# First layer's edge pass: turned one-hots of the first 16 chunks made on chip, sums cleared earlier

## What is computed

```python
x_src, x_dst, e = node_embeddings[src], node_embeddings[dst], edge_emb[edge_type]
att_in = concatenate([x_src, x_dst, e, task_rep])
edge_delta = tanh(gelu(att_in @ att_W1 + att_b1) @ att_W2 + att_b2)
edge_weight = 1.0 + edge_scale * edge_delta
...
agg = segment_sum(messages * edge_weight, dst)
deg = segment_sum(edge_weight, dst)
```

## Time and profile before

| | us |
|---|---|
| median of 3 runs | 3634.98 |
| lowest, highest | 3631.04, 3635.08 |
| profiled execution, its own time | 3634.52 |
| span of its trace | 3632.7 |
| busy: PE, DVE, ACT, POOL | 2852.6, 2641.7, 1922.9, 2197.2 |

### The profile page before, as it was taken

The page is one execution under the profiler, slowest core; times in us unless marked ns, Lnnn a source line. Parts: engine busy times, 40 slices in busy tenths (PEclk is TensorE's granted clock), DMA queues, the critical chain, the costliest instruction groups (busy, mean ns, idle before and its releaser), DMA issues. The chain is left out here.

```text
span 3632.7 us, 59741 instructions
## 1 busy us (share of the span) xinstructions
PE 2852.6 (79%) x14869; PEld 1755.7 (48%) x14869; DVE 2641.7 (73%) x7559; ACT 1922.9 (53%) x6218; POOL 2197.2 (60%) x2264
## 2 busy tenths in 40 slices
PE   2578619999989699577777768599999998888885
PEld 1444305555556455354555535466666654333332
DVE  9899828999987455688888854599999955444444
ACT  0277705555552154377777743378887844333333
POOL 0687767777767532566666523677776312777774
PEclk9988859999999699699999989799999998565665
DMA  4334337888870488877776734777777634333335
GB/s 133 115 86 124 109 96 242 265 261 265 265 202 25 116 333 341 283 219 208 213 204 203 187 106 175 213 220 220 220 221 218 157 125 185 103 103 103 103 104 102
DMA packets 259351, 651.50 MB, mean 179 GB/s; under 512 B 65353, under 2 KB 114324, under 8 KB 252244
## 3 DMA queue, kind: packets, MB, share of 16 engines
q0 software_dynamic: 143184, 474.54, 44.1%
q1 hardware_dynamic: 115844, 173.14, 14.9%
HBM read 505.48 MB, written 145.31 MB: 179 GB/s over the span
## 5 line engine op out<-in xcount | busy, mean ns | idle before, releaser
L1976 POOL DMA_INDIRECT a_rows<-table,met x568 | 549.7, 968 | 280.9 <-issue 120.0
L3537 PE MATMUL ps<-rows_in,hot_w 128*128 128x256 f32 x832 | 444.8, 644 | 104.5 <-ACT hot_w L3499 57.6
L1275 POOL DMA_INDIRECT rows_in<-table,met x416 | 411.5, 989 | 144.1 <-issue 107.1
L3487 POOL DMA_INDIRECT rows_in<-table,met x416 | 403.9, 971 | 140.6 <-issue 120.0
L3562 DVE TENSOR_TENSOR xs<-xs,ps 128x256 f32 x416 | 175.3, 421 | 303.9 <-PE ps L3537 302.1
L778 POOL DMA_INDIRECT records<-rec,rows x283 | 323.5, 1143 | 101.7 <-issue 86.0
L3537 PEld LDWEIGHTS ps<-rows_in,hot_w 128*128 128x128 f32 x832 | 196.0, 289 | 353.4 <-ACT hot_w L3499 176.9
L3499 ACT ACTIVATE hot_w<-hot,met 128x128 f32<-128x128 f32 x416 | 166.8, 402 | 374.8 <-PE ps L3537 345.6
L2452 PE MATMUL ps<-a_rows,a_hot 128*128 128x260 f32 x1136 | 314.3, 402 | 23.5 <-DVE acc L2458 16.1
L1976 POOL DMA_INDIRECT xs<-table,met x264 | 255.6, 968 | 122.9 <-issue 54.5
L2458 DVE TENSOR_TENSOR acc<-acc,ps 128x520 f32 x416 | 287.5, 691 | 20.5 <-issue 15.0
(11 more groups left out here) (473 smaller groups left out, 6422.9 us busy)
## 6 DMA issues: line engine op xcount, KB each, us to landing
a_hot_t<-one_hots SPq DMA_DIRECT2D x104, 256.0 KB, 4.8
table<-stage SPq DMA_DIRECT2D x25, 1024.0 KB, 3.9
rows_in<-table,met POOLq DMA_INDIRECT x832, 3.8
dst_row<-slot_rows SPq DMA_DIRECT2D x52, 256.0 KB, 5.2
one_hots<-hot_t SPq DMA_DIRECT2D x52, 256.0 KB, 3.6
by_dst<-lo_rows SPq DMA_DIRECT2D x24, 512.0 KB, 4.6
by_dst<-dst_rows SPq DMA_DIRECT2D x24, 512.0 KB, 5.7
a_rows<-table,met POOLq DMA_INDIRECT x568, 3.8
```

Source lines behind the costliest of these rows:

```text
L1275: e.indirect_dma_start(self.rows[:, n % self.RING, 0:2 * D], None, self.table, bass.IndirectOffsetOnAxis(ap=self.b.met[:, n, R_SRC:R_SRC + ...
L1976: e.indirect_dma_start(self.row(n, 0, self.width), None, self.table, bass.IndirectOffsetOnAxis(ap=b.met[:, n, self.word:self.word + 1], ax ...
L3487: e.indirect_dma_start(self.rows[:, n % self.RING, :], None, self.table, bass.IndirectOffsetOnAxis(ap=self.b.met[:, n, R_REL:R_REL + 1], a ...
L3537: e.matmul(b.ps[:, n % self.BANKS, 0:D], self.hot_w[:, n % GRP_H, :], self.rows[:, n % self.RING, :], start=True, stop=True).then_inc(self ...
```

## The change

The changed kernel makes `hot_t` and `kind_t` of the first 16 chunks (two groups of eight) without memory. `first_hots` compares, on VectorE, the destination and type words of eight chunks with a row of numbers, which gives the one-hots the other way round (slots along partitions), in room lent by the tile `z`; `turn_first` transposes them on TensorE, 16 transposes of a group, into two PSUM banks; `keep_first` copies the two banks into `hot_t` and `kind_t` on ScalarE. The loads of `dst_row` and `type_row` begin with the third group. `acc` is cleared before VectorE waits for the records; for that `hi_hot` and `lo_hot`, whose room it takes, are laid out first, and the clearing waits for TensorE's last use of them. The second `sources` moves behind the copies of the slot rows (`decode_rest`). Cut to its core:

```diff
-        self.hi = sb("hi_hot", [P, RC, NT], BF16)
-        self.lo_hot, self.lo_b = sb("lo_hot", [P, 2, BLK, P], BF16), sb("lo_b", [P, RC], BF16)
+        self.hi, self.lo_hot = hots
+        self.lo_b = sb("lo_b", [P, RC], BF16)
...
     FIRST_CHUNKS = 48
-    DECODED_ROWS, DECODED_FIRST, DECODED_BANKS, DECODED = 13, 16, 18, 21
+    DECODED_ROWS, DECODED_FIRST, DECODED_BANKS, DECODED = 13, 18, 22, 25
...
             e.wait_ge(self.tiles, done[0])
+        e.wait_ge(self.moved, N_BLK)
+        e.memset(self.acc[:, :, :], 0.0)
+        self.between.all_stored(e)
         e.wait_ge(*self.put.at(self.placed_before(N_BLK)))
         e.wait_ge(b.s_met, 16)
...
         assert done[0] == self.DECODED_ROWS
+        settled()
+        self.messages.first_hots(e, 0, step)
         self.sources(e, step, settled, 0, self.FIRST_CHUNKS)
         assert done[0] == self.DECODED_FIRST
+        self.messages.first_hots(e, 1, step)
         step(e.scalar_tensor_tensor(met_f[:, :, R_KEY], ps[:, 0, 0:NCH], float(P), met_f[:, :, R_DST], ALU.mult, ALU.add))
         step(e.tensor_tensor(met_f[:, :, R_W], ps[:, self.WORDS + 1, 0:NCH], qf[:, :, WEIGHT], ALU.add))
         assert done[0] == self.DECODED_BANKS
+
+    def decode_rest(self, e):
+
+        b, done, met = self.b, [self.DECODED_BANKS], self.b.met
+
+        def step(last):
+            done[0] += 1
+            last.then_inc(self.tiles, 1)
+
+        def settled():
+            e.wait_ge(self.tiles, done[0])
         self.sources(e, step, settled, self.FIRST_CHUNKS, NCH)
         assert done[0] == self.DECODED
         settled()
...
-    BANKS = 1, 2
+    BANKS = 2, 5
...
+    FIRST_GROUPS, FIRST_BANKS = 2, ((4, 3), (7, 6))
...
+        early = self.z[:, :, :, :].rearrange("p k c f -> p (k c f)").bitcast(BF16)
+        at = self.FIRST_GROUPS * GRP_T * P
+        self.early_hot = early[:, 0:at].rearrange("p (c q) -> p c q", q=P)
+        self.early_kind = early[:, at:at + self.FIRST_GROUPS * GRP_T * 3 * ET].rearrange("p (c k y) -> p c k y", k=3, y=ET)
...
-            if g >= groups:
+            if g >= groups or g < self.FIRST_GROUPS:
                 continue
...
         b, w = self.b, self.w
+        for g in range(self.FIRST_GROUPS):
+            self.keep_first(e, g)
         for t in range(self.PAIRS + 2):
...
+    def first_hots(self, e, g, step):
+
+        b, chunks = self.b, slice(g * GRP_T, (g + 1) * GRP_T)
+        word = lambda w: b.met[:, chunks, w:w + 1].bitcast(F32)
+        step(e.tensor_tensor(self.early_hot[:, chunks, :], b.iota_b[:, :].unsqueeze(1).to_broadcast([P, GRP_T, P]),
+                             word(R_DST).to_broadcast([P, GRP_T, P]), ALU.is_equal))
+        for k in range(3):
+            last = e.tensor_tensor(self.early_kind[:, chunks, k, :], b.iota_b[:, 0:ET].unsqueeze(1).to_broadcast([P, GRP_T, ET]),
+                                   word(R_TYPE).to_broadcast([P, GRP_T, ET]), ALU.is_equal)
+        step(last)
+
+    def early_bank(self, g, k, rows):
+        return self.b.ps[0:rows, self.FIRST_BANKS[g][k], :].bitcast(BF16).rearrange("p (c q) -> p c q", c=GRP_T)
+
+    def turn_first(self, e, g):
+
+        b, ranking = self.b, self.ranking
+        e.wait_ge(ranking.tiles, (ranking.DECODED_ROWS + 2, ranking.DECODED_BANKS)[g])
+        for c in range(GRP_T):
+            e.transpose(self.early_bank(g, 0, P)[:, c, :], self.early_hot[:, g * GRP_T + c, :], b.ident_b[:, :])
+            last = e.transpose(self.early_bank(g, 1, 3 * ET)[:, c, :],
+                               self.early_kind[:, g * GRP_T + c, :, :].rearrange("p k y -> p (k y)"), b.ident_b[:, :])
+        last.then_inc(self.first_turned, 1)
+
+    def keep_first(self, e, g):
+
+        e.wait_ge(self.first_turned, g + 1)
+        e.copy(self.hot_t[:, g, :, :], self.early_bank(g, 0, P)).then_inc(self.hot_t_made, 1)
+        e.copy(self.kind_t[:, g, :, :], self.early_bank(g, 1, 3 * ET)).then_inc(self.hot_t_made, 1)
...
         self.slot_rows.tensor(e, (self.ranking.tiles, self.ranking.DECODED_ROWS))
-        e.wait_ge(self.ranking.tiles, self.ranking.DECODED_BANKS)
+        for g in range(self.FIRST_GROUPS):
+            self.turn_first(e, g)
         self.ranking.between.brought(e)
         fetch(0)
         for t in range(self.PAIRS + 3):
             if t + 1 < self.PAIRS:
                 fetch(t + 1)
+            if t == 1:
+                e.wait_ge(self.slot_rows.kept, 2)
             if t % 2 and t < self.PAIRS:
...
-            e.wait_ge(self.row_in[g % 2], 32 * (g // 2 + 1))
+            e.wait_ge(self.row_in[g % 2], 32 * ((g - self.FIRST_GROUPS) // 2 + 1))
...
         self.slot_rows.vector(e)
-        e.memset(self.acc[:, :, :], 0.0)
-        turned_hots(0)
+        self.ranking.decode_rest(e)
         for t in range(self.PAIRS + 4):
-            if t % 4 == 1 and t // 4 + 1 < NCH // GRP_T:
+            if t % 4 == 1 and self.FIRST_GROUPS <= t // 4 + 1 < NCH // GRP_T:
                 turned_hots(t // 4 + 1)
...
+        hots = sb("hi_hot", [P, RC, NT], BF16, film_ctx), sb("lo_hot", [P, 2, BLK, P], BF16, film_ctx)
         film_room = sb("film_room", [P, 6 * KD * 2 * D], F32, film_ctx)
         film, load_film = film_steps(b, film_ctx, w, film_room)
-        ranks = Ranks(b, film_ctx, back, film_room[:, :])
+        ranks = Ranks(b, film_ctx, back, film_room[:, :], hots)
```

6 lines of the change are left out of this document (3 added, 3 removed).

## The result

| | us |
|---|---|
| kernel before, median of 7 runs on the same chip | 3632.74 (3629.77 to 3638.46) |
| changed kernel, median of 7 runs | 3623.42 (3619.18 to 3626.28) |
| ratio, 95% interval | 0.9971 (0.9960 to 0.9983) |
| profiled execution: time, span | 3626.28, 3624.5 |

The change is a gain of 0.29%: by the ratio 10.5 us, with an interval of 6 to 14.5. The kernel before came out 2.2 us lower here than in its first three runs. A second set of runs of the same changed kernel gave 0.9973 (0.9963 to 0.9983).

The account below looks back on a forecast made before the run. Bound: the first layer's pass, by when GpSimd's gather 16 starts after a 10.81 us pause. Gather 16 at 542.3 in place of 550.61 saves 8.3: 3634.98 - 8.3 = 3626.7 us, range 3622.5 to 3630.5.

Parts of the forecast that it names:

- a microsecond won there is a microsecond of the kernel: First layer's pass: it ends by when gather 16 starts, gathers after it taking a steady 1.296 us each.
- Product L1435 and the gather beside it: VectorE product of 0.42 us at 552.48; the gather beside it took its usual 0.94, read as not held.
- The scatter beside L320: GpSimd scatter beside VectorE's long compare: 1.90 us in place of 0.94 to 1.01, taken as the nearest case.
- Compares ahead of gather 0: Four VectorE compares before GpSimd's release: 1.9 us, moving gather 0 from 519.83 to 521.7.
- Gather 0 beside the second compares: Second four VectorE compares run while first gathers are issued: cost 0.3 us, bounds 0 and 0.95.
- The rival in which it is locked out: GpSimd held by VectorE's compares: costs 1.1 us rather than 0.3, gain 7.5, time 3627.5; chance 0.12.
- Transposes: TensorE ahead of the first fetch: four took 0.41 us, so 16 take 1.64, ending at 526.1.
- Register load of 1.37 us: TensorE, between the transposes and the first fetch: adds 1.37 us, bringing the fetch to 527.5 in place of 536.58.
- GpSimd's own queue ends last at gather 16: First place free at 541.5, before GpSimd is ready at 542.3, so the 10.81 us pause is gone.
- Rows in time for the z: VectorE's first z due at 529.9; gather 1's rows land by 529.3, close but in time.
- places come free late: Rival: rows or group 3 loads late for VectorE's z; 1 to 3 us of new pause, 3627.7 to 3629.7; chance 0.14.
- the rival of a clock that stays low: TensorE stays at 1.2 GHz, paced by gathers; the 8.3 us are lost after 3.3 pairs, kernel slower; chance 0.04.

Follow-up runs that it names:

- e3: Changed kernel with the clearing of the sums put back behind the second sources, ahead of the first z; ratio to the kernel before 0.9979.
- e6: Changed kernel with the first sources ahead of both sets of compares and each group's wide transposes before its narrow ones; ratio to the kernel before 0.9963.
- e7: Changed kernel with only the first 8 chunks' one-hots made on chip, one group in place of two; ratio to the kernel before 0.9963.
- e4: Changed kernel with each group's 8 wide transposes made first, then its 8 narrow ones, in place of in turn; ratio to the kernel before 0.9969.
- e5: Changed kernel with the first chunks' sources ahead of both sets of compares; ratio to the kernel before 0.9958.
- e2: Kernel before with only the change's early clearing of the sums and the new layout; ratio to the kernel before 1.0000.
- e1_again: Changed kernel, unedited, run once more; ratio to the kernel before 0.9973.

## Why the prediction was right, and where it was not

- **The step that failed: "a microsecond won there is a microsecond of the kernel".** Gather 16 came 8.63 us earlier (forecast 8.3), but the pass got only 7.39 shorter. That is the prediction's own sign against itself: a pass less than 8 us earlier although gather 16 came 8 us earlier. The step rested on gathers of 1.296 us, "its own duration and gap and nothing else". The gap holds (0.30 us, and behind gather 16 never over 0.6); the duration does not. It follows which of VectorE's rows the gather starts behind, and after the change 14 more were hit: gathers 16 to 415 took 2.5 us more (519.44 against 516.98). Of this 1.2 came back between the last gather and the end. Why it did is open: passes of equal length had their last gathers 0.7 us apart. In the other runs the rate isn't one for one either (e3: 2.4 later, 1.2 longer; e6: 1.3 earlier, 1.8 shorter; e7: 1.7 later, 1.5 longer). In the nine profiles of whole kernels in the first table the pass is gather 16's start and 536.7 to 538.1 us, so the start of gather 16 sets the pass to within 1.4 us, not to one.
- **The misread row behind it.** Product L1435 and the gather beside it were read as a case in which nothing is held. That gather starts 0.63 us ahead of the product, and a gather ahead of its row isn't lengthened (none of 199). The scatter beside L320 starts with 1.07 us of the compare left, and its 1.90 us are 0.947 and 1.07 less 0.13, nearly to the hundredth. Both rows say the same.
- **Compares ahead of gather 0: right.** 1.23 and 0.69 us, overlapping, delay it by 1.87 (forecast 1.9). R_W ended at 8.39 (528.26 absolute), forecast 8.65.
- **Gather 0 beside the second compares: 0.3 forecast, nothing net.** It took 1.20 us, 0.19 above its 1.01 before. But the first 16 gathers took 20.27 us as before, where one other had been lengthened to 1.15; that is luck. The rival in which it is locked out to 0.95 us past the last compare wanted its end at 527.6; it ended at 526.92. The rival's mechanism is what the rows show, but only for the row under way, and its price of 1.1 us fell.
- **Transposes: mis-sized.** "Four took 0.41, so 16 take 1.64": they took 3.69. The row has four of one width; here two widths take turns, and e6 puts 1.7 us of the difference on that alternation (2.01 us when grouped, at the same clock of 0.50; still 0.4 above the forecast).
- **Register load of 1.37 us behind them: mis-sized the other way.** The fetch started 0.15 us after the last transpose (0.22 in e6), so the loads must have run beside them. The two errors nearly cancel, which is luck: first fetch 12.29, forecast 11.65; first z 14.65, forecast 14.05. They cost nothing, since the place was needed only when GpSimd came round.
- **GpSimd's own queue ends last at gather 16: right.** 26.13, forecast 26.45 (the 0.3 above is the difference), pause gone. e4, with the fetch 2.4 us earlier, left it at 26.14.
- **Rows in time for the z: wrong for two.** The first three waited for none, the fourth and fifth waited 1.61 and 1.47 us for gathered rows. In e5 the fifth came 1.3 us earlier and the pass gained nothing. It is the rival "places come free late" as far as its mechanism goes, without its price here; in the sets with late rows it is most of the story, and the prediction had no case for them.
- **Clearing costs nothing and is needed: right.** e2 and e3 show both halves; what it is needed for is 1.2 us of the pass.
- **ScalarE, SyncE: right.** Copies 1.01 and 1.00 us (at most 1.17), and the first loads went out at 13.55, 1.3 us sooner than thought.
- **Clock: right.** Low until 25.5, forecast 25.2 (541 less 515.85), and the rival of a clock that stays low fell in the changed kernel (1.00 in the steady window). Its mechanism exists: in e4, where TensorE ran further ahead of the gathers, the clock went back to 0.50 for some 7 us.
- **The time.** 3626.7 forecast, 3623.4 measured. Of the 3.3 us 2.2 are the kernel before, which came out lower in the larger set. The saving of 8.3 lies in the measured 6 to 14.5, and the medians differ by 9.3; of these the pass gives 7.4. That the total fits is partly luck: in the two profiles the ranking ended 4.0 us later and the rest behind the pass took 4.8 us less, and e1_again (first decoding row at 515.47) shows that the later ranking isn't the change's. The other error was in calling 0.2% the line: with 7 runs each the interval was 0.12% either way, so that there is a gain could be told more easily than the chances allowed. That it is over 0.2% isn't shown (0.17 to 0.40%).

## What to carry to other kernels

Where a ring of buffers starves once, at its start, an earlier first consumer is worth what the producer's own queue leaves of the pause; past that point nothing more comes (e4), and both sides must be moved together (e6). The gain also needs the transfers to have landed by the earlier time: where the second z came 11.8 us after its gather in place of 7.0 (536.68 less 529.73), the same edit moved gather 16 by 2.4 us in place of 8.6. A queue that shows no waits still need not have a fixed pace: lay its instructions beside those of the engines that run with it, and look at which starts first. A time for a chain of small instructions should be taken from a row with the same alternation of shapes, and waits behind them should be checked for running beside them.

## What the runs showed that was not expected

- Transposes that alternate between 128 and 48 columns cost 0.226 us each at the 1.2 GHz level (0.50 granted); eight of a width in a row cost 0.12 to 0.13 each at that level (1.03 and 1.05 us for 8 in e6).
- A gather that starts behind a VectorE row whose tensors all lie in SBUF is longer by the rest of that row less 0.13 us (109 of 111 lengthened gathers of the changed kernel, within 0.02 us); one that starts ahead of the row is not.
- One and the same kernel before took 3633 us in some sets and 3988 in others, with the same work, on chip 15 both.
